# Quantised feed-forward: normalising x, rounding it and making its scales for the way back on GpSimd, ahead of the final normalisation in each step

## The reference

```
def _weight_quant(w):
    scale = 1.0 / clip(mean(abs(w)), 1e-05)
    return clip(round(w * scale), -1.0, 1.0) / scale
def _act_quant(x):
    scale = 127.0 / clip(max(abs(x), axis=-1), 1e-05)
    return clip(round(x * scale), -128.0, 127.0) / scale
def _bitlinear(x, w):
    return einsum('bsi,oi->bso', _act_quant(x), _weight_quant(w))

x = layernorm(x + cross_attention(...))
gate = silu(_bitlinear(x, w_gate))          # 128 -> 512
up = _bitlinear(x, w_up)                    # 128 -> 512
x = layernorm(x + _bitlinear(gate * up, w_down))   # 512 -> 128
```

## Time and profile before

| | |
|---|---|
| runs | 2687.25, 2696.07, 2697.22 us, median 2696.07 |
| the profiled execution | 2688.61 us, its span 2686.8 us |
| busy over the span | PE 2430.3 us (90%), DVE 2193.0 (82%), POOL 1926.0 (72%), ACT 1777.8 (66%) |
| the quantised phase | from about 2485 us to the end, 202 us |
| mean granted TensorE clock | 0.942 of full speed |

### The profile page before, as it was taken

How to read it: one execution, slowest core, us unless ns; L and a number is a source line. 1 busy time by engine, 2 the same in 40 slices (tenths; PEclk the granted TensorE clock), 3 DMA queues, 4 the chain that set the end, 5 groups by cost and what they waited for, 6 DMA issues and landing times. The chain is left out here.

```text
span 2686.8 us, 43786 instructions
## 1 busy us (share of the span) xinstructions
PE 2430.3 (90%) x13232; PEld 1512.2 (56%) x13244; DVE 2193.0 (82%) x3891; ACT 1777.8 (66%) x3501; POOL 1926.0 (72%) x1779
## 2 busy tenths in 40 slices
PE   7969999989969996899999999999989999997675
PEld 5646666656649993344444444443458787886232
DVE  5979999956645553999999999999967777777897
ACT  7847777753413335788888888787646556564997
POOL 5528999947756665799999999999736666665244
PEclk9979999989989997999999999999999999999555
DMA  5931111001128879455555555555632323322000
GB/s 148 423 110 23 23 23 22 16 14 43 42 59 227 232 201 205 173 185 212 194 200 186 209 203 194 184 214 195 226 83 84 91 82 92 89 81 67 13 25 28
DMA packets 241032, 343.66 MB, mean 128 GB/s; under 512 B 46721, under 2 KB 185494, under 8 KB 219938
## 3 DMA queue, kind: packets, MB, share of 16 engines
q1 hardware_dynamic: 217138, 316.34, 35.7%
q0 software_dynamic: 22080, 23.75, 3.8%
q10 hardware_dynamic: 1584, 0.79, 0.1%
HBM read 243.13 MB, written 98.58 MB: 127 GB/s over the span
## 5 line engine op out<-in xcount | busy, mean ns | idle before, releaser
L1887 POOL TENSOR_TENSOR s_drive<-s_du,s_b_sb 128x1024 f32<-128x1024 f32 x256 | 600.0, 2366 | 40.1 <-DVE s_state_ps L2236 39.8
L2236 DVE TENSOR_TENSOR_SCAN s_state_ps<-s_decay_ps,s_drive 128x512 f32<-128x512 f32 x416 | 485.6, 1213 | 28.5 <-ACT s_decay_ps L2033 15.4
L2033 ACT ACTIVATE s_decay_ps<-s_delta,neg_rate 128x508 f32<-128x508 f32 x512 | 342.4, 684 | 125.9 <-DVE s_state_ps L2236 71.4
L2387 PE MATMUL s_y_ps<-s_read,w_ident 128*128 128x512 f32 x832 | 393.0, 598 | 6.5 <-DVE s_read L2250 6.4
L2387 PEld LDWEIGHTS s_y_ps<-s_read,w_ident 128*128 128x128 f32 x832 | 154.6, 191 | 197.9 <-issue 165.7
L2250 DVE TENSOR_TENSOR s_read<-s_state_ps,s_c_sb 128x512 f32<-128x512 f32 x416 | 263.7, 676 | 0.0
L2689 POOL TENSOR_TENSOR c_share<-c_p,c_norm 128x1232 f32<-128x1232 f32 x64 | 148.3, 2317 | 83.3 <-DVE c_norm L2824 83.3
L1431 POOL DMA_INDIRECT m_y_scratch<-e_y,e_index x142 | 138.9, 978 | 86.2 <-DVE e_index L1467 62.6
L744 ACT ACTIVATE b_pT<-b_turn_ps 77x512 f32<-77x512 f32 x256 | 144.7, 592 | 75.8 <-PE b_turn_ps L876 75.8
L2925 PE MATMUL c_f_ps<-c_ctxT,w_c_wqk 128*128 128x308 f32 x512 | 179.2, 438 | 6.1 <-DMA c_ctxT<-in_ctxT_dram 3.2
L2317 PE MATMUL s_f_ps<-w_c_wvo,s_lotT 128*128 128x512 f32 (+1 forms) x312 | 158.0, 605 | 27.7 <-issue 16.7
(11 more groups left out here) (376 smaller groups left out, 6133.8 us busy)
## 6 DMA issues: line engine op xcount, KB each, us to landing
s_b_sb<-s_bc_scratch SPq DMA_DIRECT2D x64, 1024.0 KB, 5.0
s_c_sb<-s_bc_scratch SPq DMA_DIRECT2D x64, 1024.0 KB, 4.9
c_vp_scratch<-s_stage SPq DMA_DIRECT2D x152, 256.0 KB, 2.6
c_vp<-c_vp_scratch SPq DMA_DIRECT2D x64, 576.0 KB, 4.2
m_rows_scratch<-fill SPq DMA_DIRECT2D x33, 1040.0 KB, 27.0
e_w<-in_m_we_dram SPq DMA_DIRECT2D x71, 384.0 KB, 3.7
e_xg<-m_rows_scratch SPq DMA_DIRECT2D x71, 130.0 KB, 3.0
x<-m_y_scratch POOLq DMA_DIRECT2D x6, 768.0 KB, 15.7
```

The source lines that it names most:

```text
L1887: nc.gpsimd.tensor_tensor(drive[:, (g * states + n) % drives, :, :], du[:, s, :, :], b_sb[:, n, :].unsqueeze(1).broadcast_to([128, halves, ...
L2033: nc.scalar.activation(decay[:, m, :, 1:], delta[:, s, m, :].rearrange("p (b t) -> p b t", t=T)[:, :, 1:], ACT.Exp, scale=core.neg_rate[:, ...
L2236: nc.vector.tensor_tensor_scan(home[:, h, :], decay[:, h, :, :].rearrange("p b t -> p (b t)"), drive[:, (g * states + n) % drives, h, :], ...
L2387: last = nc.tensor.matmul(y_ps[:, m, :], core.ident[:, :], read[:, r % deep, m, :], start=False, stop=(n == states - 1))
```

## The change

In the quantised phase three functions move to POOL. `normalise` leaves ACT, `back_x` and `whole_x` leave DVE. POOL's stream becomes `step(g)`: back_x(g+1), normalise(g+4), whole_x(g+2), finish(g-1), with one wait for `shift` at its start. back_x additionally waits for `produced`, because it now runs on another engine than the product that reads the old `x_back`; peak_x waits for `back_ready` of two groups before, and the first product of a group for `back_ready` of its group.

```
@@ -3117,19 +3117,43 @@
                                                    offset[:, j:j + 1], ALU.mult, ALU.add)
                 last.then_inc(result_ready.sem, 1)
 
-            for g in range(NG):
-                finish(g)
+            def normalise(g):
+                for i in range(g * GB, (g + 1) * GB):
+                    last = nc.gpsimd.tensor_scalar(x[:, i, :], x[:, i, :], core.rstd[:, i:i + 1], shift[:, i:i + 1],
+                                                   ALU.mult, ALU.add)
+                last.then_inc(x_normed.sem, 1)
+
+            def back_x(g):
+                pool.wait_ge(x_steps.sem, x_steps.at(g, 2))
+                if g >= 2:
+                    pool.wait_ge(silu_ready.sem, silu_ready.at(2 * g - 3, 2))
+                    pool.wait_ge(produced.sem, produced.at(2 * g - 3, 2))
+                nc.gpsimd.tensor_tensor(x_back[:, g % 2, :, :], x_top[:, g % 2, :].unsqueeze(2).broadcast_to([128, GB, 2]),
+                                        w_mean[:, 0:2].unsqueeze(1).broadcast_to([128, GB, 2]),
+                                        ALU.mult).then_inc(back_ready.sem, 1)
+
+            def whole_x(g):
+                pool.wait_ge(scaled.sem, scaled.at(g, 1))
+                if g >= 1:
+                    pool.wait_ge(x_turned.sem, x_turned.at(g - 1, 1))
+                nc.gpsimd.tensor_scalar(xq[:, :, :], x_scaled[:, :, :], core.to_whole, 127.0, ALU.subtract,
+                                        ALU.min).then_inc(xq_ready.sem, 1)
+
+            def step(g):
+                if on(g, 1, NG):
+                    back_x(g + 1)
+                if on(g, 4, NG):
+                    normalise(g + 4)
+                if on(g, 2, NG):
+                    whole_x(g + 2)
+                if on(g, -1, NG):
+                    finish(g - 1)
+
+            pool.wait_ge(shifted.sem, shifted.at(0, 1))
+            around(pool, step)
 
         @block.scalar
         def _(act):
-            def normalise(g):
-                if g == 0:
-                    act.wait_ge(shifted.sem, shifted.at(0, 1))
-                for i in range(g * GB, (g + 1) * GB):
-                    last = nc.scalar.activation(x[:, i, :], x[:, i, :], ACT.Identity, bias=shift[:, i:i + 1],
-                                                scale=core.rstd[:, i:i + 1])
-                last.then_inc(x_normed.sem, 1)
-
             def rescale_x(g):
                 act.wait_ge(x_steps.sem, x_steps.at(g, 3))
                 act.wait_ge(x_normed.sem, x_normed.at(g, 1))
@@ -3177,8 +3201,6 @@
                             rescale_h(k, s, e)
                     if s == 0 and on(g, 2, NG):
                         rescale_x(g + 2)
-                    if s == 1 and on(g, 4, NG):
-                        normalise(g + 4)
                     if on(k, 0):
                         copy_h(k, 0)
                     if s == 1 and on(g, 2, NG):
@@ -3195,6 +3217,8 @@
 
             def peak_x(g):
                 dve.wait_ge(x_normed.sem, x_normed.at(g, 1))
+                if g >= 2:
+                    dve.wait_ge(back_ready.sem, back_ready.at(g - 2, 1))
                 nc.vector.tensor_reduce(x_top[:, g % 2, :], x[:, g * GB:(g + 1) * GB, :], AX.X, ALU.max,
                                         apply_absolute_value=True).then_inc(x_steps.sem, 1)
                 dve.wait_ge(x_steps.sem, x_steps.at(g, 1))
@@ -3205,23 +3229,10 @@
                     dve.wait_ge(scaled.sem, scaled.at(g - 2, 1))
                 nc.vector.reciprocal(x_scale[:, g % 2, :], x_top[:, g % 2, :]).then_inc(x_steps.sem, 1)
 
-            def back_x(g):
-                dve.wait_ge(x_steps.sem, x_steps.at(g, 2))
-                if g >= 2:
-                    dve.wait_ge(silu_ready.sem, silu_ready.at(2 * g - 3, 2))
-                nc.vector.tensor_tensor(x_back[:, g % 2, :, :], x_top[:, g % 2, :].unsqueeze(2).broadcast_to([128, GB, 2]),
-                                        w_mean[:, 0:2].unsqueeze(1).broadcast_to([128, GB, 2]),
-                                        ALU.mult).then_inc(back_ready.sem, 1)
-
-            def whole_x(g):
-                dve.wait_ge(scaled.sem, scaled.at(g, 1))
-                if g >= 1:
-                    dve.wait_ge(x_turned.sem, x_turned.at(g - 1, 1))
-                nc.vector.tensor_scalar(xq[:, :, :], x_scaled[:, :, :], core.to_whole, 127.0, ALU.subtract,
-                                        ALU.min).then_inc(xq_ready.sem, 1)
-
             def product(k, g, s, e):
                 dve.wait_ge(silu_ready.sem, silu_ready.at(k, e + 1))
+                if s == 0 and e == 0:
+                    dve.wait_ge(back_ready.sem, back_ready.at(g, 1))
                 if behind(k, 2):
                     dve.wait_ge(hq_ready.sem, hq_ready.at(k - 2, e + 1))
                 nc.vector.scalar_tensor_tensor(h[:, s, e, :], u_ps[:, e, :], x_back[:, g % 2, 2 * s + e, 1:2],
@@ -3278,16 +3289,12 @@
                             whole_h(k, s, e)
                     if on(k, 1):
                         scales_h(k + 1, 1 - s)
-                    if s == 0 and on(g, 1, NG):
-                        back_x(g + 1)
                     if s == 1 and on(g, 3, NG):
                         peak_x(g + 3)
                     if on(k, -1):
                         leave(k - 1, g - 1 + s, 1 - s)
                     if on(k, 1):
                         back_h(k + 1, 1 - s)
-                    if s == 0 and on(g, 2, NG):
-                        whole_x(g + 2)
 
             around(dve, step)
 
```

## The result

The changed kernel takes 2698.67 us (median of 19 runs) against 2692.43 for the kernel before (19 runs beside them): a ratio of 1.0024, 95% interval [1.0016, 1.0032], 4.3 to 8.6 us slower. That is inside the half per cent taken as no change, and the forecast of 2698 met it. The difference behind it doesn't fit as well: +1.8 us was summed up, +6.5 was measured (by the ratio; the medians are 6.2 apart). (The three runs that the forecast started from had a median 3.6 us above that of the 19.)

What follows compares the result with a forecast made beforehand. DVE was taken to bound the first half-step, a loop through DVE, PE and ACT the second. Terms 1.2 + 0.6 + 0 = +1.8 us gave 2690.4, plus 7.46 to the runs' median, 2698; range 2686 to 2713.

Steps and rivals of the forecast that it cites:

- The loop: Second half-step: rounding of h on DVE, turning on PE, copy and gate on ACT, product on DVE; 2.33 us.
- F: Faster rival, chance 0.08: the loop shortens, DVE's relief counts in full, steps of 10.56 us, total 2687.
- DVE sets the first half-step: First half-step, product to product: 5.88 us with no gap found on DVE.
- POOL's price of whole_x: whole_x on POOL taken as 1.04 us, from a two-input operation of its size; ends 0.42 and 1.78.
- Start in all: Start of the phase: +1.2 us before the first xq, +0.6 for DVE waiting in the first step.
- Lock-step of POOL and DVE: First half-step: gain up to 0.15 us or loss about 0.3 per step; taken as 0, range -2 to +4.
- signs of being right: DVE's share down some 0.5 us a step, ACT's 1.6; step 11.2 to 11.6; gate wait some 0.7; POOL about 8.
- Rival B: Slower rival, chance 0.24: whole_x precedes the rounding of h every step, about 1.0 us each, total 2711.
- The dead heat: Second half-step: POOL could start whole_x at 2582.37, DVE's rounding of h at 2582.34; ACT up to 0.11 earlier.
- L3201 loses its 0.15, which sets the rounding earlier: First half-step: x's small scaling on DVE freed of 0.15 us as result writes run later; argued against Rival B.
- P: Rival, chance 0.03: POOL becomes the bound, whole_x at 4.3 us or more; at 5.2, some 2710.
- The gate's wait: Second half-step: DVE's product waits for ACT's gate, 0.17 us growing to some 0.7, up to 0.75; gain 0.

Runs made afterwards that it cites:

- e1: The change with whole_x back on DVE, normalise and back_x staying on POOL; 2692.46 us, ratio 1.0004 to the kernel before.
- e4: The change with whole_x on POOL as four instructions of 128x128 instead of one of 128x512; 2691.17 us, ratio 0.9999 to the kernel before.
- e13: The kernel before with half of the peak's reduction moved to the second half-step, nothing on POOL; 2686.60 us, ratio 0.9985 to the kernel before.
- e8: The change with whole_x in four pieces and the first two groups' whole_x on DVE; 2689.83 us, ratio 0.9996 to the kernel before.
- e2: The change with normalise back on ACT, whole_x and back_x staying on POOL; 2691.98 us, ratio 1.0003 to the kernel before.
- e12: The change with normalise waiting for back_h of the same half-step, whole_x in one piece; 2693.40 us, ratio 1.0008 to the kernel before.
- e11: As e8, with half of the peak's reduction moved from the first half-step to the second; 2687.73 us, ratio 0.9990 to the kernel before.
- e16: As e13, with back_x alone of the change put on POOL; 2685.49 us, ratio 0.9981 to the kernel before.
- e15: As e11, with normalise waiting for back_h; 2688.66 us, ratio 0.9986 to the kernel before.
- e3: The change with POOL's whole_x waiting for the rounding of h; 2693.64 us, ratio 1.0008 to the kernel before.

## Why the prediction was right, and where it wasn't

- **The loop sets the second half-step, so relief of DVE and ACT there is worth nothing: right.** In e1, with normalise and back_x gone from ACT and DVE, it is 5.42, in e4, with whole_x gone too, 5.44, as at the end of the phase. F falls.
- **DVE sets the first half-step: right**, and the runs add its other side: 0.40 us taken off DVE *there* (e13) came off each of the 13 steps, 5.2 us, of which the second half-step (5.50 for 5.43) gave 0.9 back.
- **POOL's price of whole_x, "I take 1.04": wrong**, 1.94, and above the end of 1.78 from the four result writes. The nearest row had f32 out; whole_x writes bf16, and in e8 a piece of 128x128 with bf16 out takes 0.638 us at best, where a normalise of that size, a different operation with f32 out, takes 0.456. The Trainium skill, page "GPSIMD Engine Reference", section "Elementwise — side-by-side cycle accounting", gives 769 ns for 512 one-input elements at best; this instruction takes 2.5 times that. At the start the first product came 1.92 us later (10.34 to 12.26 behind the shift), not 1.2, but the rounding behind whole_x lost 0.15 instead of 0.6. Start in all: 2.09 for 1.8.
- **"Lock-step of POOL and DVE: I take 0, since both ends move against each other": the step that failed.** It is +4.74 us over 13 steps, beyond the +4 of its range. The gain that it named came (-0.10 in x's scaling). Of the losses, the hold of back_h by normalise was not seen at all, and that of the rounding by whole_x stood with the rivals. Of the prediction's signs of being right, the step (11.2 to 11.6; it is 11.82) and DVE's share (some 0.5 less; it is 0.06 more) didn't come.
- **Rival B happened, at a third of its price.** The dead heat went to POOL in 12 of 14 cases; "L3201 loses its 0.15, which sets the rounding earlier" didn't decide it. But the hold is 0.36 us, not 1.0. In all 23 cases of the change, e2 and e12 in which a whole_x of one piece led a rounding (by 0.02 to 0.43 us), that rounding ended 0.88 to 0.90 us after whole_x's start. Unheld it takes 0.42, so the way was free about 0.47 after the start, with 1.47 of whole_x still to run. The Trainium skill, page "SBUF — State Buffer", section "SBUF: two separate sides", says that the first holds the shared ports for its whole instruction. That whoever starts first wins, the traces of e12 bear out; that the hold lasts for the whole instruction doesn't agree with 0.47 of 1.94.
- **P falls:** POOL idles some 2 us in each steady step ahead of whole_x, at 8.86 us of work (8.0 was summed up; whole_x is the difference).
- **The gate's wait**, 0.17 to 0.61, came as forecast and for its reason: back_x leaves room for 0.11 us on DVE (with it alone gone, in e1, the wait is 0.28) and whole_x for 0.33, less than the 0.58 that their durations add up to. The hold adds nothing to it, since it sets the gate and DVE's work behind the rounding later alike.

So the forecast of "no change" was right because the loop hides what is taken from DVE and ACT, and its size was off by 4.7 us because POOL's instructions hold two of DVE's that nothing hides. That the forecast of 2698 came within 1 us is luck: the sum was over 4 us short, and the median that it was added to was 3.6 us high. Left open: why whole_x takes 1.94, and what sets the length of a hold (below).

## What to carry to other kernels

Before moving work off a busy engine, see in which stretch its work, and not a loop through other engines, sets the end: here moving half a reduction from one half-step to the other, on the same engine, won 4 us where moving whole operations to another engine lost 6.5. Work that goes to GpSimd beside a busy VectorE is priced by what it holds there: a shorter instruction held less in these traces (0.16 us against 0.47), and a hold in a place where VectorE waits anyway cost nothing (the small scaling in e2). Its order counts as much, since a change of one operation moves all that stand behind it on GpSimd (e4, e11). And when one engine is relieved, look for the next that sets the end (ACT in e16). A hold that depends on who starts first by 0.1 us can't be forecast from order alone; the range has to take both.

## What had not been expected of the hardware

The hold is shorter than GpSimd's instruction, and no fixed share of it. Its end can be read where a DVE instruction started behind one of GpSimd's: the end of that DVE instruction less the time that it takes unheld.

| GpSimd's instruction | takes, us | DVE came free, us after its start | where |
|---|---|---|---|
| whole_x, 128x512, bf16 out | 1.94 | 0.47 | the 23 roundings of h above |
| a piece of it, 128x128, bf16 out | 0.64 | 0.15 to 0.17 | roundings in e8, e11 and e15, back_h in e4, e8, e11 and e15 |
| a piece of normalise, 128x128, f32 out | 0.45 | 0.31 to 0.36 | all held back_h of the change and e1; five roundings in e15 |
| the same, itself held up by the rounding | 0.73 | 0.15 to 0.16 | eight roundings in e3 |
| a result write, 128x128, f32 out | 0.45 | 0.31 | back_h in e11 |

The piece of normalise with back_h behind it, in the steady step of the change:

```profile
2574.53 0.45 POOL L3122 TENSOR_SCALAR x<-x,rstd,q_shift 128x128 f32<-128x128 f32 x1
```

```profile
2574.62 0.36 DVE L3263 TENSOR_TENSOR q_h_back<-q_h_top,q_w_mean 128x2 f32<-128x2 f32 x1
```

A rounding that started 0.25 us behind the first of four pieces wasn't held at all, and one that started 0.05 behind was held for 0.10 (a single one, in e11, at 0.02 behind, wasn't held). The lines of e8, for each of the two POOL's first piece and then DVE's rounding of h:

```profile
2562.24 0.81 POOL L3140 TENSOR_SCALAR q_xq<-q_x_scaled 128x128 bf16<-128x128 f32 x1 [0.73 <-ACT q_x_scaled L3165]
...
2640.39 0.71 POOL L3140 TENSOR_SCALAR q_xq<-q_x_scaled 128x128 bf16<-128x128 f32 x1 [2.40 <-ACT q_x_scaled L3165]
```

```profile
2562.49 0.42 DVE L3258 TENSOR_SCALAR q_hq<-q_h 128x512 bf16<-128x512 f32 x1
...
2640.45 0.52 DVE L3258 TENSOR_SCALAR q_hq<-q_h 128x512 bf16<-128x512 f32 x1
```

What short pieces alone are worth in the steps isn't shown, since e4 and e8 changed the order with them. And VectorE can hold GpSimd in turn: where the rounding came first, whole_x took 2.09 instead of 1.94, and the pieces above took 0.71 and 0.81 instead of 0.64.
